# Last layer of a routed expert network: 10 shared tiles, 38 slot tiles, 6 shared tiles

## What is computed

```python
gate = xt @ Wr + br
_, ids = jax.lax.top_k(gate + gate_bias, 2)
probs = softmax of gate over the two chosen experts
u = jnp.einsum('nh,ehi->eni', xt, Wup) + bup[:, None, :]
g = silu(jnp.einsum('eni,eij->enj', u, Wgate) + bgate[:, None, :]) * u
eo = jnp.einsum('enj,ejh->enh', g, Wdown) + bdown[:, None, :]
out = jnp.einsum('ne,enh->nh', probs, eo)
su = xt @ Wsu + bsu
so = (silu(su @ Wsg + bsg) * su) @ Wsd + bsd
out = out + so
```

## Time and profile before

| | us |
|---|---|
| three runs | 1003.20, 1005.99, 1006.02 |
| median | 1005.99 |
| the profiled execution: its own time | 1003.24 |
| its span, first to last instruction | 1001.4 |
| mean granted TensorE clock, share of 2.4 GHz | 0.851 |

### The profile page before, as it was taken

How to read it: one execution, slowest core, us unless ns; L and a number is a source line. 1 busy time by engine, 2 the same in 40 slices (tenths; PEclk the granted TensorE clock), 3 DMA queues, 4 the chain that set the end, 5 groups by cost and what they waited for, 6 DMA issues and landing times. The chain is left out here.

```text
span 1001.4 us, 17388 instructions
## 1 busy us (share of the span) xinstructions
PE 825.4 (82%) x4556; PEld 512.4 (51%) x4556; DVE 656.4 (66%) x1554; ACT 418.6 (42%) x916; POOL 333.1 (33%) x588
## 2 busy tenths in 40 slices
PE   0599997666666879898898998889998889999990
PEld 0445554233332335566766875446666745666650
DVE  8598995789975866655822226768887676544445
ACT  0457663455541331222225772456666223333330
POOL 2000004143327661202773772300002286134330
PEclk9799998765557989655599998999999679999995
DMA  9301008999104019704153543410000322223217
GB/s 328 90 22 22 21 8 263 313 315 323 38 0 140 1 42 324 203 0 169 69 175 104 159 125 106 158 26 20 19 15 9 129 87 79 69 77 93 84 46 251
DMA packets 90419, 113.22 MB, mean 113 GB/s; under 512 B 11573, under 2 KB 82008, under 8 KB 89194
## 3 DMA queue, kind: packets, MB, share of 16 engines
q1 hardware_dynamic: 83578, 95.46, 31.6%
q0 software_dynamic: 6768, 16.86, 4.7%
HBM read 51.36 MB, written 58.42 MB: 110 GB/s over the span
## 5 line engine op out<-in xcount | busy, mean ns | idle before, releaser
L761 ACT ACTIVATE probs_t<-ps 128x1024 f32<-128x1024 f32 x64 | 65.5, 1024 | 72.5 <-PE ps L1648 72.5
L606 POOL COPY work<-ctx_rows 128x256 f32 (+1 forms) x32 | 12.7, 400 | 215.7 <-PE ps L1659 215.7
L1107 DVE TENSOR_REDUCE row_max<-ps 128x8 f32<-128x1024 f32 x64 | 77.8, 1216 | 5.0 <-PE ps L1638 2.5
L1113 DVE TENSOR_TENSOR work<-ps,row_max 128x1024 f32<-128x1024 f32 x64 | 77.7, 1214 | 3.4
L1490 DVE TENSOR_TENSOR ctx_cols<-ps,ctx_rows 128x512 f32<-128x512 f32 x54 | 37.3, 691 | 59.9 <-PE ps L2050 59.7
L973 ACT ACTIVATE ctx_cols<-ctx_cols 128x256 f32<-128x256 f32 x54 | 22.5, 417 | 117.3 <-DVE ctx_cols L1490 113.9
L2050 PE MATMUL ps<-early,xt 128*128 x152 | 71.5, 593 | 0.0
L755 ACT ACTIVATE work<-work 128x1024 f32<-128x1024 f32 x64 | 67.2, 1050 | 7.5 <-DVE work L1113 7.5
L1648 PE MATMUL ps<-ident,work 128*128 128x128 f32 x512 | 69.1, 278 | 1.4 <-ACT work L755 1.4
L583 POOL DMA_INDIRECT y_rows<-ctx_cols,w2d x38 | 37.5, 988 | 80.7 <-DMA y_rows<-ctx_cols,w2d 47.1
L1648 PEld LDWEIGHTS ps<-ident,work 128*128 128x128 f32 x512 | 56.0, 141 | 15.3 <-ACT work L755 10.1
(11 more groups left out here) (334 smaller groups left out, 1990.8 us busy)
## 6 DMA issues: line engine op xcount, KB each, us to landing
x_rows<-pad_row SPq DMA_DIRECT2D x1, 17415.0 KB, 68.2
work<-x_rows SPq DMA_DIRECT2D x77, 129.0 KB
x_rows<-pad_row SPq DMA_DIRECT2D x1, 7740.0 KB, 33.2
x_rows<-pad_row SPq DMA_DIRECT2D x1, 7611.0 KB, 38.3
early<-in_w3st SPq DMA_DIRECT2D x8, 512.0 KB
work<-y_rows SPq DMA_DIRECT2D x16, 256.0 KB, 3.0
early<-y_rows SPq DMA_DIRECT2D x8, 512.0 KB, 7.4
late<-in_w2u SPq DMA_DIRECT2D x1, 2304.0 KB, 45.3
```

Source lines behind the costliest of these rows:

```text
L761: act.activation(probs_t[:, :, :], ps[:, 4:6, :], ACT.Copy).then_inc(sem("att.evac"), 1)
L1107: dve.tensor_reduce(row_max[:, u, 8 * c:8 * c + 8], scores(c), AX.X, ALU.max).then_inc(sem("att.max"), 1)
L1113: dve.tensor_tensor(probs[:, u, c, :].rearrange("p (h k) -> p h k", k=P), scores(c), row_max[:, u, 8 * c:8 * c + 8].unsqueeze(2).to_broadc ...
```

## The change

The work list of the last layer becomes 10 shared tiles (steps 0 to 9), 38 slots (steps 10 to 47), 6 shared tiles (steps 48 to 53), on PE, ACT and DVE alike. The output banks, buffers and semaphore counts follow the step number. SP may load `y_rows3` once the up products of all slots are issued, except the last load, which lies over the shared expert's weights and waits for all 54. DVE does the first eight of the 32 mixing operations inside the loop, at the end of step 52; each mixing operation also waits for its tile's `add_shared`. The gated bias is added in five instructions, for tiles 0 to 3, 4 to 7, 8 and 9, 10 and 11, 12 to 15. The sending by POOL, with its copies between the scatters, isn't touched.

```diff
+NS3 = 10
+def work3(i):
+
+    if i < NS3:
+        return i, None
+    if i < NS3 + N3:
+        return None, i - NS3
+    return (i - N3 if i < NT + N3 else None), None
...
@@ SP @@
-            upto(sp, "m3.up", NT + N3)
+            upto(sp, "m3.up", NS3 + N3)
...
                 for k in range(2):
+                    if g == NG - 1 and k:
+                        upto(sp, "m3.up", NT + N3)
                     sp.dma_start(yc[:, k, 4 * g:4 * g + 4, :], yr3[:, k, 4 * g:4 * g + 4, :]).then_inc(sem(f"load.x{g}"), 16)
...
@@ ACT @@
-                s = i + 1 - NT
-                if 0 <= s < N3:
+                s = work3(i + 1)[1]
+                if s is not None:
                     upto(act, "s3.tr", s + 1)
                     if s >= 2:
-                        upto(act, "m3.up", NT + s - 1)
+                        upto(act, "m3.up", NS3 + s - 1)
...
@@ DVE @@
+            def returned(g):
+                dve.wait_ge(sem(f"load.x{g}"), 16 + 32)
+                for k in range(2):
+                    for t in range(4 * g, 4 * g + 4):
+                        upto(dve, "m3.added", t + 1)
+                        if k:
+                            upto(dve, "mixed", 8 * g + t - 4 * g + 1)
+                        dve.scalar_tensor_tensor(x[:, t, :], yc[:, k, t, :], wk[k][:, t:t + 1], x[:, t, :], ALU.mult, ALU.add
+                                                 ).then_inc(sem("mixed"), 1)
...
-                if 2 <= i < NT + 2:
-                    if i % 4 == 2:
-                        xg = x[:, i - 2:i + 2, :]
-                        seq(dve.tensor_tensor(xg, xg, b_dn_gated.unsqueeze(1).to_broadcast([P, 4, D]), ALU.add))
-                    add_shared(i - 2)
-                elif i >= NT + 2:
-                    out_slot(i - 2 - NT, expert[i - 2])
+                if i >= 2:
+                    t, s = work3(i - 2)
+                    if s is not None:
+                        out_slot(s, expert[i - 2])
+                    else:
+                        if t % 4 == 0 or t == NS3:
+                            xg = x[:, t:min(NT if t >= NS3 else NS3, t + 4 - t % 4), :]
+                            n = xg.shape[1]
+                            seq(dve.tensor_tensor(xg, xg, b_dn_gated.unsqueeze(1).to_broadcast([P, n, D]), ALU.add))
+                        add_shared(t, i - 2)
                 if 3 <= i < NT + N3:
                     hidden(i)
+                if i == NT + N3 - 2:
+                    returned(0)
...
-            upto(dve, "m3.added", NT)
-            for g in range(NG):
-                dve.wait_ge(sem(f"load.x{g}"), 16 + 32)
...
+            for g in range(1, NG):
+                returned(g)
...
@@ PE @@
             for i in range(NT + N3 + 2):
-                if NT <= i + 1 < NT + N3:
-                    if i + 1 == NT:
+                t, s = work3(i)
+                after = work3(i + 1)[1]
+                if after is not None:
+                    if after == 0:
                         upto(pe, "rt3.read", NG + 1)
-                    turn_slot(3, i + 1 - NT, xd3)
-                if i < NT:
-                    if i < 2:
-                        pe.wait_ge(sem("rt3.gate"), i + 1)
+                    turn_slot(3, after, xd3)
+                if t is not None:
+                    if t < 2:
+                        pe.wait_ge(sem("rt3.gate"), t + 1)
                     expert[i] = E3
-                    up3(i, cols(xt_all, i), E3)
-                elif i < NT + N3:
-                    upto(pe, "s3.x", i - NT + 1)
-                    up3(i, xt[:, (i - NT) % 2], expert[i])
+                    up3(i, cols(xt_all, t), E3)
+                elif s is not None:
+                    upto(pe, "s3.x", s + 1)
+                    up3(i, xt[:, s % 2], expert[i])
```

More of the change, by code:

```diff
@@ L1498, in out_slot, with add_shared @@
             def out_slot(s, e):
-                upto(dve, "m3.down", NT + s + 1)
+                upto(dve, "m3.down", NS3 + s + 1)
                 if s >= 4:
                     dve.wait_ge(sem(f"back{s % 4}"), loads(N2, 4, s % 4) + 16 * (s // 4))
[L1502 to L1506, removed]
+                dve.tensor_tensor(y3[:, s % 4], bank(4 + (NS3 + s) % 2, D), b_dn[:, e], ALU.add).then_inc(sem("s3.y"), 1)
+            def add_shared(t, i):
+                upto(dve, "m3.down", i + 1)
+                dve.scalar_tensor_tensor(x[:, t, :], bank(4 + i % 2, D), tg[:, 7:8], x[:, t, :], ALU.mult, ALU.add
                                          ).then_inc(sem("m3.added"), 1)
@@ L1542, in _ @@
                               ).then_inc(sem("rt3.sub"), 1)
+            def returned(g):
[7 more added lines that the diff above has]
+                                                 ).then_inc(sem("mixed"), 1)
             expert = {}
             for i in range(NT + N3 + 2):
-                if NT <= i + 1 < NT + N3:
-                    if i + 1 == NT:
+                s = work3(i + 1)[1]
+                if s is not None:
+                    if s == 0:
                         dve.wait_ge(sem("b3.load"), 32)
                         upto(dve, "rt3.eid", 1)
-                    expert[i + 1] = dve.value_load(eid3[0:1, i + 1 - NT:i + 2 - NT], min_val=0, max_val=E3 - 1)
+                    expert[i + 1] = dve.value_load(eid3[0:1, s:s + 1], min_val=0, max_val=E3 - 1)
                 if 3 <= i < NT + N3:
                     sums(i, expert.get(i, E3))
-                if 2 <= i < NT + 2:
-                    if i % 4 == 2:
-                        xg = x[:, i - 2:i + 2, :]
-                        seq(dve.tensor_tensor(xg, xg, b_dn_gated.unsqueeze(1).to_broadcast([P, 4, D]), ALU.add))
-                    add_shared(i - 2)
-                elif i >= NT + 2:
-                    out_slot(i - 2 - NT, expert[i - 2])
+                if i >= 2:
+                    t, s = work3(i - 2)
+                    if s is not None:
+                        out_slot(s, expert[i - 2])
[5 more added lines that the diff above has]
+                        add_shared(t, i - 2)
                 if 3 <= i < NT + N3:
                     hidden(i)
+                if i == NT + N3 - 2:
+                    returned(0)
                 if i == 10:
@@ L2062, in down3 @@
                 upto(pe, "m3.ht", i + 1)
[L2063 to L2066, removed]
-                else:
-                    upto(pe, "rt3.read", i + 3)
+                if i < 2:
+                    upto(pe, "rt3.read", i + 3)
+                else:
+                    t, s = work3(i - 2)
+                    if s is not None:
+                        upto(pe, "s3.y", s + 1)
+                    else:
+                        upto(pe, "m3.added", t + 1)
                 for j in range(2):
@@ L2089, in _ @@
                     totals(3, E3, run3)
-                if NT <= i + 1 < NT + N3:
-                    if i + 1 == NT:
+                if after is not None:
+                    if after == 0:
                         upto(pe, "rt3.eid", 1)
-                    expert[i + 1] = pe.value_load(eid3[0:1, i + 1 - NT:i + 2 - NT], min_val=0, max_val=E3 - 1)
+                    expert[i + 1] = pe.value_load(eid3[0:1, after:after + 1], min_val=0, max_val=E3 - 1)
                 if i == 1:
```

## The result

The changed kernel takes 1010.75 us, the median of 20 runs (1006.23 to 1013.79), the kernel before 1002.9 us in its 20 runs (998.43 to 1006.22). The ratio is 1.0075, 95% interval 1.0062 to 1.0088: slower by 7.5 us by the ratio, 7.85 us by the two medians. The prediction was +6.3 us, 1012.3 us, range 1008 to 1016.

The account below looks back on a forecast made before the run. PE was taken to bound the layer, so order could change only its two edges. Terms 13.1 + 2.6 - 0.8 - 8.6 = +6.3 us, on the 1005.99 us median, gave 1012.3 us, range 1008.0 to 1016.0.

Parts of the forecast that it names:

- The stall: Last layer, step 9: PE waits at the first slot transpose until the slot's rows land at 850.0; +13.1 us.
- The clock: Behind the stall PE resumes at 0.50 and loses half of a 5.30 us low stretch; +2.6 us (1.7 to 4.3).
- slower still: Rival: copy stays slow, clock falls a second time after the restart, first returned pair lands late; +10.3 us, chance 0.15.
- The softmax step: Step 10: most of the 1.1 us PE loses to DVE's eight softmax-weight operations vanishes; -0.8 us (0 to -1.1).
- The tail: Last edge: PE ends 3.0 us later, but 13.5 us instead of 25.15 stand behind it; -8.6 us.
- signs of being wrong: First slot landing before 845, PE at 1.00 at once, or PE's end and last mixing over 11 us apart.
- what the next profile was to show: Some 13 us PE idle, clock 0.50 briefly then 1.00 to PE's end, no 3.9 us step, PE end near 994.
- Near nothing: Rival: eight mixing operations hold up nobody, tail gains in full, clock costs only 1.7; +2.4 us, chance 0.11.
- faster: Rival: with DVE silent POOL's pairs shrink and the stall shortens, tail gains in full; -5.9 us, chance 0.03.

Follow-up runs that it names:

- y2: Changed kernel without its last eight pairs of copy and scatter, the mixing reading first-choice rows instead; ratio to the kernel before 0.9944.
- y3: Changed kernel with 14 shared tiles ahead of the slots and 2 behind, all mixing behind the loop; ratio to the kernel before 0.9989.
- x1: Kernel before with token numbers copied for four tiles in one instruction, then four scatters back to back, last layer only; ratio to the kernel before 1.0189.
- x2: Changed kernel with token numbers copied for four tiles at once, then four scatters back to back, last layer only; ratio to the kernel before 1.0127.
- y1: Changed kernel with 14 extra unused products on PE ahead of the first slot transpose; ratio to the kernel before 1.0061.
- x4: Changed kernel with the first eight mixing operations one step later, behind the hidden product of step 53; ratio to the kernel before 1.0041.
- y4: Changed kernel with the first eight mixing operations one step later and the softmax-weight operations in step 8 instead of 10; ratio to the kernel before 1.0027.
- z3: Changed kernel with four-tile grouped copies and a one-column scratch copy, with signal and wait, between scatters; ratio to the kernel before 1.0079.
- z2: Changed kernel with token-number copies for two tiles at a time, so at most two last-layer scatters stand back to back; ratio to the kernel before 1.0040.
- x3: Changed kernel with 28 extra unused products on PE ahead of the first slot transpose; ratio to the kernel before 1.0168.

## Why the prediction was right

**The stall** was predicted at 13.1 us and measured at 13.0, for the reasons given: the last copy didn't grow, since DVE's addition came after the stall, and the landing was at 850.5 where 850.0 was said (with the layer starting 0.9 us later). y2 shows the price by removing it. One reading behind it was too narrow: that a scatter takes 0.97 or 0.98 us and only a copy grew. In the same layer of the kernel before three scatters took 1.07 to 1.20 us and two more copies 1.01 and 1.24. And where a scatter, not a copy, falls beside DVE's long bias addition, it is the scatter that grows, as in y3:

```profile
847.82 1.26 DVE L1584 TENSOR_TENSOR x<-x,work 128x1024 f32<-128x1024 f32 x1
...
848.27 1.65 POOL L554 DMA_INDIRECT x_rows<-late,w2d  x1 [0.28 <-POOL late L551]
```

It ends 849.92 - 849.08 = 0.84 us behind the addition. One in x1 (1.62 us) and one in x2 (1.44 us) do the same, each 0.83 us behind it.

**The clock** was +2.6, bounds 1.7 to 4.3; measured 2.0 in the step behind the stall, and 1.95 by y1. Three other profiles with the whole stall (x4, y4, z3) give 1.8 to 2.2. I took the row of the longer low stretch, 5.30 us; behind the stall the granted clock was 0.50 until 854.5, thus for about 4 us, and half of that is 2.0. The right mechanism, a size near the lower bound. But it fell a second time, at the end, which I had priced only in the rival *slower still*, and for another place.

**The softmax step** was -0.8 and came out at 0: this step failed. It rested on step 10 running at the low clock. The clock was back by 855.8, when step 10 began, and the long step (861.87 to 866.02) lost 1.13 us as before. The bias addition in step 10 did take 0.68 us instead of 1.22, but DVE then stood 0.78 us between the eight operations and its next large one at 863.05, where before it went straight on; what it waited for the runs don't show. y4 takes the loss away.

**The tail** was -8.6 and came out at -7.1. The order of events was right: the data was there in time, the first of the two last down products started 2.7 us later behind the last up product than before (3.0 predicted; PE's wait ahead of it was 3.37), and the mixing queued behind the last shared addition. What the term left out is that PE, idle through the hold-up, does its last products at the low level, 2.08 us each instead of 1.13. With that PE ended 11.4 us after its last up product, where 9.65 were predicted (6.65 before and the 3.0). The end behind PE, 13.35 us, was predicted at 13.5.

The four errors (-0.1, -0.6, +0.8, +1.5) add up to +1.6; less 0.3 of small things that takes +6.3 to +7.6, against +7.7 measured. Part of the fit is thus luck: two errors of +0.8 and +1.5 stand against two of -0.1 and -0.6. The absolute time is luck in part too. 1012.3 was reckoned from 1005.99, the median of three runs; over twenty the kernel before takes 1002.9, from which the same +6.3 gives 1009.2, and the measured 1010.75 lies between the two. Of the signs of being wrong none came; of what the next profile was to show, three things didn't: the clock did not stay at 1.00 to PE's end, a step of 4.15 us remained, and PE ended at 996.65, not near 994. *Near nothing* needed a tail in full, which x4 shows to exist but one step later; *faster* needed a pair of about 0.5 us, and the pair stayed at 1.44 with DVE silent.

The Trainium skill, page SBUF — State Buffer, section "A bandwidth-pool intuition that's wrong (but worth ruling out)", gives about 620 ns for a DMA alone whose descriptors GpSimd writes. In the silent stall here the scatters took 0.96 to 1.00 us [the POOL rows above]. The measurement decides: against the usual 0.97 there was nothing to gain from DVE's silence. Beside DVE's long addition one took 1.65 us, as shown above.

## What to carry to other kernels

Moving covered work to another place pays only as far as its old place had slack: here 3.8 us of six tiles' 18 us, and the rest of the cover turned into a wait almost one for one, with two microseconds of low clock on top. Four tiles fewer behind the slots (y3) meant no stall and no low clock. Ask of work put between a loop's last steps who waits behind it in the same queue; one step later was worth 3.4 us here. And measure a queue's pace with its gaps before taking an instruction's length for it.

## What the runs showed that was not expected

Four scatters in a row on POOL, with only 0.30 us between them, went with ACT and DVE standing up to 10.9 us for signals of PE (one of them taken up 15 us after PE's work was done), two in a row with up to 4.1 us; with a copy and its wait between every two, there were none. The trace does not say what held them up, and no run here separates the missing copy, the missing wait and the faster pace.

A hold-up of 3.4 us near the end cost the clock: the granted value is 1.00 from 988.30 to 990.30, with PE idle, and 0.50 in the stretch of the last down products. It varied between executions: both of them ran at the low level in the profiles of after, y2 and z2, the second alone in those of y1 and x2, and in x3 and z3 the second and, in part, the first (1.48 and 1.49 us). In x4, y3 and y4, where the eight operations don't stand there, neither did.
